# Dealing the row-maximum tiles of a cross-attention kernel otherwise over the steps of its windows

## The chip, the core and the metric

The kernel runs on one core of a Trainium2 chip. The time is device time in microseconds (us) of that core. Lower is better.

## What is computed

Two layers follow each other. The first, on `x` (8 sequences of 56 tokens of width 128) and a context (8 sequences of 1500 rows), is self-attention, cross-attention to the context, and a mixture of 8 experts with the best 2 of them chosen. The second is one more cross-attention to the same context, with weights rounded to three values. The core of both cross-attentions, with 16 heads of width 8, is:

```
k = context @ Wk.T + bk ; v = context @ Wv.T + bv        # 1500 rows for each of 8 sequences
scores = einsum('bqhd,bkhd->bhqk', q, k) * SCALE
probs  = softmax(scores, axis=-1)
out    = einsum('bhqk,bkhd->bqhd', probs, v)
```

## The kernel before, in words

All engines are programmed by hand, each with its own straight list of instructions, and wait for each other by semaphores. Each of the two cross-attentions is a *pass* over the 8 sequences (*units*). A pass has 8 *windows*, one for each unit, and a window has 12 *steps* k = 0 to 11. I write a window as (pass, unit): (0, 3) or (1, 0). Between the passes stand the experts.

In step k TensorE first computes one block of **scores** (`scores`, L1343, 8 matmuls into the PSUM tensor ST); ScalarE takes its exponential (`exp_step`, L671). In even steps TensorE then multiplies the exponentials of the two steps before with the **values** (`values`, L1386, 32 matmuls into PO).

The softmax needs the maximum of every score row ahead of the exponentials. So, one window ahead, the scores of the next unit are computed once more in rough form: 24 **max tiles** of 112 x 500 (`max_tile`, L1371). Each goes into one of the two banks of SM, and VectorE reduces it to its row maximum (`reduce_tile`, L883). A tile may only be computed when the reduction of the tile two before it is done. The tiles are numbered 0 to 23. How many stand in which step is the table `STEP_TILES`; the first window of all, (0, 0), has a table of its own, and the last window of each pass has no tiles. When tile 11 or tile 23 is reduced, `max_parts` makes the negated maxima of half the rows, and TensorE turns them (`transpose_max`, L1308) right after the scores of step 6 or of step 1.

Besides, a window prepares later units through one PSUM bank, MI. In steps 0, 1, 2 it projects the keys of the unit two ahead (`project_k`, L1282; thirds of 500 columns). ScalarE reads each third twice (`kf`, L635, then `ksplit`, L636), and the next third may be projected only after that. GpSimd then computes a rest (`k_rest`, L527), VectorE rounds it (`k_second_part`, L878, one in each of the steps 1, 2, 3), and GpSimd computes the third part (`k_third_part`, L532). In steps 4, 5, 6 the values of the next unit are projected (`project_v`, L1292). Step 7 turns the attention output back (`output_back`, L1318), which VectorE divides by the row sums in step 8 (L918). In pass 0, steps 9, 10, 11 transpose context (`transpose_ctx`, L1271, windows 0 to 4), and VectorE takes statistics of context in steps 5 to 10. In pass 1 the transposed context comes from HBM instead (`load_xT`, L368).

The three places for tiles within one step are: the first tile behind the values (behind the scores in odd steps), the middle ones directly behind it, the last one behind the projection.

SyncE's queue moves data between windows: `place` (L428) and `restack` (L412, six transfers that stack the rounded keys into `kst`), and `load_qall` (L393), which spreads the queries when they are split. A wait in this queue holds up all behind it.

Of the kernel before, what the change touches and what calls it, by code (L numbers as in the profile page):

```python
# [75 lines left out]
def spread_tiles(own, per):  # L76

    tiles = [(0, j) for j in range(TILES - own, TILES)] + [(1, j) for j in range(TILES)]
    assert sum(per) == len(tiles)
    return [tiles[sum(per[:k]):sum(per[:k + 1])] for k in range(STEPS)]  # L80
# [3 lines left out]

STEP_TILES = spread_tiles(0, (3, 3, 3, 2, 2, 2, 2, 2, 1, 1, 2, 1))
OWN_MX_STEP, NEXT_MX_STEP = 1, 6
# [5 lines left out]
OUT_AT, LN_AT, ROUTER_AT, GATES_AT, B2_AT = (5, 10), (6, 10), (6, 11), (7, 9), (7, 11)  # L92
LN5_AT, Q2_AT = (1, 3), (1, 9)
SPLIT2_AT = ((1, 10), (1, 11), (2, 0))
TERNARY_AT = ((4, 5), (4, 6), (4, 7), (4, 9), (4, 10), (4, 11), (5, 4), (5, 5), (5, 6), (5, 7), (5, 9))
# [77 lines left out]
def build_kernel(nc, x_in, ctx_in, ctxT_in, watt_in, vec_in, rows_in, rwT_in, w1T_in, w2T_in, b2_in,  # L173
                 ident_in, mask_in, out):
    with ExitStack() as ctx:
# [175 lines left out]
        def _(sp):  # L351
# [79 lines left out]
            def window(n):  # L431
# [4 lines left out]
                if n.s == 0 and n.c == B - 1:  # L436
                    restack(nxt, 1)
                if n.s == 0 and (n + 4).exists():
                    load_ctx(n + 4)
# [4 lines left out]
                if xT_unit is not None and xT_unit.s == 1:  # L444
                    load_xT(xT_unit)
                if n.s == 1 and n.c == 1:
                    load_qall(2)
                if n.s == 0 and n.c in (3, 4):
# [342 lines left out]
        def _(dve):  # L791
# [234 lines left out]
            def window(n):  # L1026
# [4 lines left out]
                for k in range(STEPS):  # L1031
                    tiles = n.tiles(k)
# [29 lines left out]
                    if n.s == 0 and (n.c, k) == GATES_AT:  # L1062
                        copy_gates(0)
                    if n.s == 1 and (n.c, k) == (0, 9):
                        token_stats(5)
                    if n.s == 1 and (n.c, k) == (0, 11):
                        token_normalise(5)
                    if n.s == 1 and (n.c, k) == LN5_AT:
                        token_gain(5)
# [127 lines left out]
        def _(pe):  # L1197
# [193 lines left out]
            def window(n, prev):  # L1391
# [3 lines left out]
                for k in range(STEPS):  # L1395
                    scores(n, k)
                    tiles = [(n + ahead, j) for ahead, j in n.tiles(k)]
                    if k % 2 == 0 and (k or prv.exists()):
                        of = n if k else prv
                        values(of, (k - 2) % STEPS)  # L1400
                        values(of, (k - 1) % STEPS)
                    if tiles:
                        max_tile(*tiles[0])
                    for tile in tiles[1:-1]:
# [271 lines left out]
```

## Time and profile before

| | us |
|---|---|
| three runs | 573.84, 576.63, 576.68 |
| median | 576.63 |
| the profiled execution | 574.07 |
| its span, first to last instruction | 572.3 |

| engine | busy, share of the span |
|---|---|
| TensorE (PE) | 90% |
| VectorE (DVE) | 68% |
| ScalarE (ACT) | 58% |
| GpSimd (POOL) | 39% |

TensorE's granted clock is 0.962 of full speed in the mean, and 1.00 in all the windows. PEld is TensorE's weight load, which overlaps the matmuls. A matmul's row gives its start and its duration to the last result; the next one starts earlier, so TensorE's time is best read from start to start.

### The profile page before, as it was taken

Reading aid. Unit: us, or ns where it says so; the run is one execution under the profiler, and the core shown is the slowest. Engines: PE = TensorE matmul, PEld = TensorE weight load, DVE = VectorE, ACT = ScalarE, POOL = GpSimd, SP = SyncE. Lnnn points to the kernel's source line nnn. Section 1 sums busy time; section 2 is a strip of 40 time slices with the busy share of each in tenths; the row PEclk is TensorE's granted clock in tenths of the full one; section 3 lists DMA queues with packets and bytes.
Section 4 is the critical chain, followed back from the end, with each engine's and each line's share of the span. In section 5 each row is a group of like instructions: output and inputs, shape, how many; then the busy total and the mean of one; then the engine's idle time right before and its main releaser. Section 6 shows DMA issues by size and latency. Waiting matters only on the chain.

```text
span 572.3 us, 16262 instructions
## 1 busy us (share of the span) xinstructions
PE 514.1 (90%) x6648; PEld 386.4 (68%) x6648; DVE 390.0 (68%) x976; ACT 334.4 (58%) x527; POOL 221.3 (39%) x217
## 2 busy tenths in 40 slices
PE   3599748889999999999989999999998999999996
PEld 2588515466767767676767998877666676766774
DVE  5666378788887888787741434887867777786730
ACT  1166223557676777776576444376666667675573
POOL 3659744475777768423160200031404033140000
PEclk9799677899999999999999999999999999999998
DMA  5110552634354554555638401006354835535200
GB/s 160 48 55 3 143 122 50 169 89 132 95 139 112 143 145 101 137 120 143 182 73 223 141 2 31 2 1 154 72 150 113 201 92 140 144 85 121 56 4 9
DMA packets 37869, 58.69 MB, mean 103 GB/s; under 512 B 17956, under 2 KB 21404, under 8 KB 37796
## 3 DMA queue, kind: packets, MB, share of 16 engines
q1 hardware_dynamic: 37476, 57.60, 39.8%
q8 instruction: 53, 0.87, 0.6%
q14 instruction: 20, 0.16, 0.1%
q10 hardware_dynamic: 320, 0.06, 0.1%
HBM read 17.81 MB, written 0.23 MB: 32 GB/s over the span
## 4 chain that ended last, share of the span: by engine, by line
PE 68%; DVE 17%; POOL 4%; DMA 3%; issue 3%; ACT 2%; SPq 2%; DVEq 0%; ACTq 0%; POOLq 0%
PE PO L1386 14%; PE SM L1371 14%; DVE mxp L883 11%; PE ST L1343 10%; PE MI L1292 8%; PE ST L1564 4%; PE ST L1554 4%; PE MI L1282 3%; PE MI L1271 2%; POOL cxs L518 2%; PE MI L1318 2%; DMA xT<-in_ctxT 1%; ACT pts L671 1%; PE SM L1477 1%; SPq L393 1%
## 5 line engine op out<-in xcount | busy, mean ns | idle before, releaser
L883 DVE TENSOR_REDUCE mxp<-SM 112x1 f32<-112x500 f32 x374 | 241.0, 673 | 74.4 <-PE SM L1371 73.2
L671 ACT ACTIVATE pts<-ST 128x896 f32<-128x896 f32 x192 | 171.7, 913 | 31.3 <-PE ST L1343 30.8
L1371 PE MATMUL SM<-kst,qst 96*112 96x500 bf16 x374 | 142.2, 399 | 13.0 <-DVE mxp L883 9.0
L527 POOL TENSOR_TENSOR kr<-kf,ksplit 128x500 f32<-128x500 f32 x48 | 55.1, 1150 | 172.4 <-ACT ksplit L636 172.4
L1343 PEld LDWEIGHTS ST<-qst,kst 98*128 98x128 bf16 x1536 | 95.8, 100 | 29.5 <-issue 4.7
L1343 PE MATMUL ST<-qst,kst 98*128 98x112 bf16 x1536 | 106.9, 213 | 2.6 <-DMA qst<-mrow 2.6
L1386 PE MATMUL PO<-pts,vaug 125*32 125x112 f32 x3072 | 97.3, 263 | 2.3 <-ACT pts L671 1.9
L1371 PEld LDWEIGHTS SM<-kst,qst 96*112 96x112 bf16 x374 | 45.6, 129 | 61.5 <-DVE mxp L883 45.0
L1386 PEld LDWEIGHTS PO<-pts,vaug 125*32 125x32 f32 x3072 | 69.3, 109 | 14.8 <-ACT pts L671 5.7
L518 POOL TENSOR_SCALAR cxs<-cxs,cmv,crstd 125x128 f32<-125x128 f32 x84 | 67.4, 819 | 0.0
L532 POOL TENSOR_TENSOR ksplit<-kr,ksplit 128x500 bf16<-128x500 f32 x48 | 54.4, 1135 | 16.9 <-DVE ksplit L878 16.9
L648 ACT ACTIVATE vaug<-MI 125x512 f32<-125x512 f32 x48 | 28.7, 598 | 53.1 <-PE MI L1292 53.1
L1292 PEld LDWEIGHTS MI<-watt,xT 128*125 128x125 f32 x384 | 50.6, 193 | 4.1 <-ACT vaug L648 1.4
L1292 PE MATMUL MI<-watt,xT 128*125 128x128 f32 x384 | 52.4, 281 | 1.1 <-DVE hT L827 0.8
L635 ACT ACTIVATE kf<-MI,vec 128x500 f32<-128x500 f32 x46 | 31.2, 678 | 36.0 <-PE MI L1282 35.7
L1282 PE MATMUL MI<-xT,watt 128*128 128x500 f32 x92 | 48.1, 604 | 1.5 <-ACT ksplit L636 0.8
L769 ACT ACTIVATE moe<-ST,vec 128x224 f32<-128x224 f32 x64 | 28.5, 448 | 34.8 <-PE ST L1554 33.9
L878 DVE CAST ksplit<-kr 128x500 bf16<-128x500 f32 x48 | 35.0, 729 | 10.2 <-POOL kr L527 10.1
L636 ACT ACTIVATE ksplit<-MI,vec 128x500 bf16<-128x500 f32 x46 | 30.8, 670 | 0.0
L623 ACT ACTIVATE xT<-MI,vec 128x500 f32<-128x500 f32 x24 | 18.4, 767 | 16.5 <-PE MI L1271 16.4
L506 POOL TENSOR_TENSOR xrstd<-xvar,half_neg 112x2 f32<-112x2 f32 (+1 forms) x6 | 4.9, 811 | 59.5 <-DVE xvar L809 59.5
L511 POOL TENSOR_TENSOR crstd<-cvar,half_neg 125x12 f32<-125x12 f32 x8 | 18.3, 2289 | 18.0 <-DVE cvar L865 18.0
(156 smaller groups left out, 539.8 us busy)
## 6 DMA issues: line engine op xcount, KB each, us to landing
kst<-ksplit SPq DMA_DIRECT2D x192, 187.5 KB, 3.6
cxs<-in_ctx SPq DMA_DIRECT2D x8, 750.0 KB
xT<-in_ctxT SPq DMA_DIRECT2D x8, 750.0 KB, 6.5
qst<-qall SPq DMA_DIRECT2D x56, 21.0 KB, 1.9
watt<-in_watt SPq DMA_DIRECT2D x1, 768.0 KB, 5.5
cxs<-in_w1T SPq DMA_DIRECT2D x3, 256.0 KB, 5.7
cxs<-in_w2T SPq DMA_DIRECT2D x3, 256.0 KB, 6.3
pts<-in_w1T SPq DMA_DIRECT2D x3, 256.0 KB, 5.4
```

What stands on the lines that cost most here:

```text
L518: last = nc.gpsimd.tensor_scalar(cx[n.par][:, c], cx[n.par][:, c], cmv[n.par][:, c, 0:1], crstd[n.par][:, c:c + 1], ALU.subtract, ALU.mult)
L527: nc.gpsimd.tensor_tensor(kr[:, c], kf[:, c], ksplit[n.par][:, 0, c], ALU.subtract).then_inc(kr_done, 1)
L532: nc.gpsimd.tensor_tensor(ksplit[n.par][:, 2, c], kr[:, c], ksplit[n.par][:, 1, c], ALU.subtract).then_inc(k3_done, 1)
L635: nc.scalar.activation(kf[:, c], bank[:, 0:THIRD], ACT.Identity, bias=bias_k(n.s + 1)).then_inc(k_evac, 1)
L671: nc.scalar.activation(PT[:, k % PTB], ST[:, k % 2, :, 0:4 * PC], ACT.Exp, scale=SCALE).then_inc(exp_done, 1)
L878: nc.vector.tensor_copy(ksplit[n.par][:, 1, c], kr[:, c]).then_inc(k2_done, 1)
L883: nc.vector.tensor_reduce(mxp[:, j // 3, j % 3:j % 3 + 1], tile_bank(j, banks), AX.X, ALU.max).then_inc(sm_red, 1)
L1282: mm(bank[:, 0:THIRD], watt[:, n.s + 1, 1], xT[n.par][:, THIRD * i:THIRD * (i + 1)], start=True, stop=True).then_inc(kp_full, 1)
L1292: last = mm(MI[0:KC, D * c:D * (c + 1)], xT[n.par][:, at:at + KC], watt[:, n.s + 1, 2], start=True, stop=True)
L1343: last = mm(ST[:, k % 2, cc, PC * p:PC * (p + 1)], kst[n.par][:, 4 * half + p, at:at + 128], qst[n.par][:, 4 * half + p], start=True, stop ...
L1371: mm(tile_bank(j, banks), qst[n.par][0:SROWS, j // 3], kst[n.par][0:SROWS, j // 3, at:at + THIRD], start=True, stop=True).then_inc(sm_full, 1)
L1386: last = mm(PO[32 * p:32 * p + 32, PC * half:PC * (half + 1)], vaug[n.par][:, c, at:at + 32], PT[0:KC, k % PTB, cc, PC * p:PC * (p + 1)], ...
```

## The change

Three things are changed, and nothing is computed otherwise.

1. The table: the 24 tiles are dealt 3, 2, 3, 1, 3, 2, 3, 2, 2, 1, 1, 1 to the steps, where they were dealt 3, 3, 3, 2, 2, 2, 2, 2, 1, 1, 2, 1. The table of window (0, 0) stays.
2. The order in a step: the first tile is computed ahead of the values, directly behind the scores. With at most three tiles in a step, one stands behind the scores, one behind the values and one behind the projection, where there are such.
3. In the second pass: the layer norm of the second half of the tokens, which precedes their query projection, moves from window (1, 1), step 3, to (1, 0), step 10, its parts on VectorE from steps 9 and 11 to 4 and 9; the query projection itself moves from (1, 1), step 9, to step 10; and SyncE issues `load_qall(2)` later, behind the first `restack` of window (1, 2) instead of at the end of window (1, 1).

```diff
--- before.py
+++ after.py
@@ -82,7 +82,7 @@
 
 
 
-STEP_TILES = spread_tiles(0, (3, 3, 3, 2, 2, 2, 2, 2, 1, 1, 2, 1))
+STEP_TILES = spread_tiles(0, (3, 2, 3, 1, 3, 2, 3, 2, 2, 1, 1, 1))
 OWN_MX_STEP, NEXT_MX_STEP = 1, 6
 FIRST_TILES = spread_tiles(TILES - START_TILES, (3, 3, 3, 3, 2, 2, 3, 3, 2, 2, 2, 2))
 FIRST_OWN_MX_STEP, FIRST_NEXT_MX_STEP = 3, 8
@@ -90,8 +90,8 @@
 
 
 OUT_AT, LN_AT, ROUTER_AT, GATES_AT, B2_AT = (5, 10), (6, 10), (6, 11), (7, 9), (7, 11)
-LN5_AT, Q2_AT = (1, 3), (1, 9)
-SPLIT2_AT = ((1, 10), (1, 11), (2, 0))
+LN5_AT, Q2_AT = (0, 10), (1, 10)
+SPLIT2_AT = ((1, 11), (2, 0), (2, 1))
 TERNARY_AT = ((4, 5), (4, 6), (4, 7), (4, 9), (4, 10), (4, 11), (5, 4), (5, 5), (5, 6), (5, 7), (5, 9))
 TAIL_BACK, TAIL_FORTH, TAIL_OUT, TAIL_LN, TAIL_ROUTER, TAIL_GATES, TAIL_B2 = 1, 3, 5, 9, 11, 18, 20
 TAIL_EXP, V0_PLACE = 15, 10
@@ -435,6 +435,8 @@
                     restack(n + 1, 1)
                 if n.s == 0 and n.c == B - 1:
                     restack(nxt, 1)
+                if n.s == 1 and n.c == 2:
+                    load_qall(2)
                 if n.s == 0 and (n + 4).exists():
                     load_ctx(n + 4)
                 if (n + 2).exists():
@@ -443,8 +445,6 @@
                     restack(k_unit, 0)
                 if xT_unit is not None and xT_unit.s == 1:
                     load_xT(xT_unit)
-                if n.s == 1 and n.c == 1:
-                    load_qall(2)
                 if n.s == 0 and n.c in (3, 4):
                     load_expert(n.c - 3)
                 if n.s == 0 and n.c >= 5:
@@ -1061,11 +1061,11 @@
                         router_gates(0)
                     if n.s == 0 and (n.c, k) == GATES_AT:
                         copy_gates(0)
+                    if n.s == 1 and (n.c, k) == (0, 4):
+                        token_stats(5)
                     if n.s == 1 and (n.c, k) == (0, 9):
-                        token_stats(5)
+                        token_normalise(5)
                     if n.s == 1 and (n.c, k) == (0, 11):
-                        token_normalise(5)
-                    if n.s == 1 and (n.c, k) == LN5_AT:
                         token_gain(5)
                     if n.s == 1 and (n.c, k) in SPLIT2_AT:
                         split_q(2, (SPLIT2_AT.index((n.c, k)),))
@@ -1395,12 +1395,12 @@
                 for k in range(STEPS):
                     scores(n, k)
                     tiles = [(n + ahead, j) for ahead, j in n.tiles(k)]
+                    if tiles:
+                        max_tile(*tiles[0])
                     if k % 2 == 0 and (k or prv.exists()):
                         of = n if k else prv
                         values(of, (k - 2) % STEPS)
                         values(of, (k - 1) % STEPS)
-                    if tiles:
-                        max_tile(*tiles[0])
                     for tile in tiles[1:-1]:
                         max_tile(*tile)
                     if 0 <= k - K_STEP < 3 and k_unit is not None:
```

On TensorE, steps 1 and 2 of window (0, 1), before. L1343 are scores, L1371 max tiles, L1282 the key projection, L1386 the values:

```order
L1343 MATMUL ST<-qst1,kst1 128x112 x8
L1308 MATMUL ST<-identb,mparts 8x112
L1371 MATMUL SM<-kst0,qst0 112x500 x2
L1282 MATMUL MI<-xT1,watt 128x500
L1371 MATMUL SM<-kst0,qst0 112x500
L1343 MATMUL ST<-qst1,kst1 128x112 x8
L1386 MATMUL PO<-pts,vaug1 32x112 x16
L1371 MATMUL SM<-kst0,qst0 112x500 x2
L1282 MATMUL MI<-xT1,watt 128x500
```

The same place after the change:

```order
L1343 MATMUL ST<-qst1,kst1 128x112 x8
L1308 MATMUL ST<-identb,mparts 8x112
L1371 MATMUL SM<-kst0,qst0 112x500
L1282 MATMUL MI<-xT1,watt 128x500
L1371 MATMUL SM<-kst0,qst0 112x500
L1343 MATMUL ST<-qst1,kst1 128x112 x8
L1371 MATMUL SM<-kst0,qst0 112x500
L1386 MATMUL PO<-pts,vaug1 32x112 x16
L1371 MATMUL SM<-kst0,qst0 112x500
L1282 MATMUL MI<-xT1,watt 128x500
```

Between the key projections of step 1 and step 2 the tiles now stand one by one; ahead of the projection of step 1 there is one tile where there were two.

On VectorE, steps 1 to 4 of window (0, 4), before. L878 are the three castings of the key rest in steps 1, 2, 3, L883 the reductions of the tiles, L889 the start of `max_parts`:

```order
L878 CAST ksplit<-kr 128x500
L883 TENSOR_REDUCE mxp<-SM 112x1 x3
L878 CAST ksplit<-kr 128x500
L883 TENSOR_REDUCE mxp<-SM 112x1 x2
L878 CAST ksplit<-kr 128x500
L883 TENSOR_REDUCE mxp<-SM 112x1 x2
L889 TENSOR_REDUCE nmx<-mxp 112x4
```

And after:

```order
L878 CAST ksplit<-kr 128x500
L883 TENSOR_REDUCE mxp<-SM 112x1 x3
L878 CAST ksplit<-kr 128x500
L883 TENSOR_REDUCE mxp<-SM 112x1
L878 CAST ksplit<-kr 128x500
L883 TENSOR_REDUCE mxp<-SM 112x1 x3
L889 TENSOR_REDUCE nmx<-mxp 112x4
```

Ahead of the third casting there is one reduction where there were two, and behind it, up to `max_parts`, there are three where there were two.

On SyncE's queue, at the seam of the windows (1, 1) and (1, 2):

```order
 L412 DMA kst<-ksplit 16x4x1500 x6
 L368 DMA xT<-in_ctxT 128x1500
-L393 DMA qall<-qsplit 16x8x224 x6
 L428 DMA qst<-qall 48x4x56 x2
 L412 DMA kst<-ksplit 16x4x1500 x6
+L393 DMA qall<-qsplit 16x8x224 x6
 L428 DMA qst<-qall 48x4x56 x2
```

The six issues of `load_qall` are moved past the two of `place` and the six of `restack`.

## Rows read from the trace of the kernel before

**Rows 1.** The page, chain of work that ended last: share of the span by engine.

```profile
PE 68%; DVE 17%; POOL 4%; DMA 3%; issue 3%; ACT 2%; SPq 2%; DVEq 0%; ACTq 0%; POOLq 0%
```

**Rows 2.** The waits: engine, line, waited for, us in total, times, longest.

```profile
PEld SM L1371 <- DVE mxp L883: 45.0, 119, 1.6
```

**Rows 3.** Timeline of window (0, 3), TensorE: start, us, instruction; in brackets idle before.

```profile
182.74 0.56 PE L1343 MATMUL ST<-qst,kst 98*128 98x112 bf16 x8
183.23 0.97 PE L1386 MATMUL PO<-pts,vaug 125*32 125x112 f32 x32
184.14 0.63 PE L1371 MATMUL SM<-kst,qst 96*112 96x500 bf16 x2
184.61 1.00 PE L1282 MATMUL MI<-xT,watt 128*128 128x500 f32 x2
...
190.22 1.00 PE L1282 MATMUL MI<-xT,watt 128*128 128x500 f32 x2
...
191.27 0.56 PE L1343 MATMUL ST<-qst,kst 98*128 98x112 bf16 x8
...
195.23 0.56 PE L1343 MATMUL ST<-qst,kst 98*128 98x112 bf16 x8
195.80 0.42 PE L1371 MATMUL SM<-kst,qst 96*112 96x500 bf16 x1
...
204.44 0.65 PE L1271 MATMUL MI<-ident,cxs 125*128 125x125 f32 x4 [0.64 <-DVE on L918]
...
208.74 0.46 PE L1343 MATMUL ST<-qst,kst 98*128 98x112 bf16 x6
```

**Rows 4.** Timeline of the same window, all engines, around its third key projection.

```profile
191.83 0.67 ACT L636 ACTIVATE ksplit<-MI,vec 128x500 bf16<-128x500 f32 x1
...
192.39 1.73 ACT L671 ACTIVATE pts<-ST 128x896 f32<-128x896 f32 x2
...
192.65 1.14 POOL L527 TENSOR_TENSOR kr<-kf,ksplit 128x500 f32<-128x500 f32 x1 [0.69 <-ACT ksplit L636]
...
193.75 1.14 POOL L532 TENSOR_TENSOR ksplit<-kr,ksplit 128x500 bf16<-128x500 f32 x1
193.82 1.33 DVE L878 CAST ksplit<-kr 128x500 bf16<-128x500 f32 x1 [0.17 <-POOL kr L527]
...
195.08 1.25 DVE L883 TENSOR_REDUCE mxp<-SM 112x1 f32<-112x500 f32 x2
```

**Rows 5.** Timeline of window (1, 4), TensorE: the scores of steps 0, 5 and next 0.

```profile
474.86 0.56 PE L1343 MATMUL ST<-qst,kst 98*128 98x112 bf16 x8
...
487.55 0.56 PE L1343 MATMUL ST<-qst,kst 98*128 98x112 bf16 x8
...
499.00 0.56 PE L1343 MATMUL ST<-qst,kst 98*128 98x112 bf16 x8
```

**Rows 6.** Timeline of the windows (1, 0) and (1, 1), all engines.

```profile
386.58 0.56 PE L1343 MATMUL ST<-qst,kst 98*128 98x112 bf16 x8
...
392.83 1.30 SPq L368 DMA_DIRECT2D xT<-in_ctxT  x1
...
400.33 1.08 PE L1282 MATMUL MI<-xT,watt 128*128 128x500 f32 x2 [0.70 <-DMA xT<-in_ctxT]
...
402.75 0.30 PEld L1282 LDWEIGHTS MI<-xT,watt 128*128 128x128 f32 x2 [0.23 <-ACT ksplit L636]
...
426.99 1.00 PE L1282 MATMUL MI<-xT,watt 128*128 128x500 f32 x2
```

**Rows 7.** Timeline of window (1, 2), all engines.

```profile
431.84 4.24 SPq L412 DMA_DIRECT2D kst<-ksplit  x6
...
439.25 0.39 PE L1371 MATMUL SM<-kst,qst 96*112 96x500 bf16 x1 [1.68 <-issue]
```

**Rows 8.** Timeline at the seam of windows (0, 0) and (0, 1).

```profile
130.76 0.56 PE L1343 MATMUL ST<-qst,kst 98*128 98x112 bf16 x8
...
131.06 1.26 DVE L883 TENSOR_REDUCE mxp<-SM 112x1 f32<-112x500 f32 x2
```

## The prediction

> **What bounds the kernel now.** The chain of work that ended last lies 68% on TensorE and 17% on VectorE [rows 1]. So TensorE is the bound, and VectorE stands in its way in places; the list of waits says where: weight loads of max tiles waited 45.0 us in 119 pieces for reductions [rows 2]. Part of that is hidden, since a weight load overlaps the matmul before it. What counts is read from start to start in the timeline.
>
> Window (0, 3) starts at 182.74 and the next at 208.74, a period of 26.00; its step 5 begins 12.49 after its start [rows 3]. In pass 1 the period is 24.14, and step 5 begins after 12.69 [rows 5]. TensorE's prices, from the same rows: scores and values together 1.40 (182.74 to 184.14), so about 0.49 for scores ahead of values and 0.91 for values; two tiles 0.47, so 0.24 each; a key projection with one tile 1.05. Scores ahead of a tile cost 0.40 (the tile at 195.80 stands 0.57 behind its scores, and 0.17 of that I read as waiting for a reduction). At 204.44 TensorE waited 0.64 for the division of step 8.
>
> Eleven windows are regular: (0, 1) to (0, 6) and (1, 2) to (1, 6). (0, 0) has its own table, (1, 0) and (1, 1) the layer norm, and the last of each pass no tiles.
>
> **The change part by part.** *The order and the table, first half of a window.* I walk through it with those prices, from the first scores at 0. Scores, tile, values, tile: 0.40 + 0.24 + 0.91 + 0.24 = 1.79, and the first key projection starts (before: 1.87). The second now has only scores, the turning of the maxima and one tile ahead of it, so TensorE is there early, but MI must be emptied first. The second reading starts 1.61 after a projection and takes 0.67 [rows 4], so this is possible 2.3 after the first one. The trace shows this limit once: at 402.75, 2.42 after the projection at 400.33, the weight load waited for ksplit [rows 6]. Hence 4.09. To the third: 1.05 + 0.40 + 0.24 + 0.91 + 0.24 = 2.84, hence 6.93. It was at 7.48 [rows 3], so 0.55 is gained so far.
>
> It is lost again on two other engines. ScalarE's exponentials of steps 3 and 4 start 2.17 after the third projection and take 1.73 together [rows 4], so the first is there at 10.0, while TensorE, with one tile in step 3, would want it 0.3 to 0.4 sooner. Then VectorE: it reaches the third casting with one reduction less behind it and has nothing to do until GpSimd has the rest ready; the casting then takes 1.33, since GpSimd's next instruction started 0.07 ahead of it, and the next reduction starts 4.86 after the third projection (190.22 to 195.08) [rows 4]. That does not move with the tiles. So the reduction of tile 9 starts at 11.79 and ends at 12.46, tile 11 starts at 12.50 where TensorE alone would be there at about 11.65, and step 5 begins at 12.74. That is 0.25 later than before in pass 0, 0.05 in pass 1.
>
> The Trainium skill, "SBUF — State Buffer", section "SBUF: two separate sides", says that VectorE and GpSimd share a port pair by an exclusive lock and that whichever instruction starts first holds it to its end. By that rule a casting that won the 0.07 us race would not be held at all; I make that a rival below, priced from rows.
>
> *Second half.* One tile moves there (12 stand ahead of step 5, where there were 13). In all it costs 0.24 of TensorE. The wait of 0.17 at 195.80 falls away. In pass 0 the 0.64 at 204.44 goes too, since two tiles and the values stand between; but VectorE has one more reduction there, beside its statistics, and I put new waits at 0.4 (bounds: 0, and the 0.64 itself). The sum is +0.07 in pass 1 and -0.17 in pass 0, where the context is transposed.
>
> So a regular window changes by +0.12 in pass 1 (five), +0.08 in (0, 1) to (0, 4), about +0.25 in (0, 5) and (0, 6), which have no transposes to gain from: 0.6 + 0.3 + 0.5 = **+1.4 us**. The bounds for one window: with no wait at all TensorE would be at step 5 after 11.1 (1.79, then 1.9 and 2.84 to the second and third projection, and 4.6 for one more with its tile, two scores, values, three tiles and a value projection), a gain of 1.4 to 1.6; if nothing is gained in the second half, loss 0.5.
>
> *The seam of (0, 0) and (0, 1).* Tiles of (0, 0) are still being reduced: VectorE starts two at 131.06 [rows 8]. Tile 0 now stands right behind the scores, at 131.16, and needs the first of these, done at 131.73. Formerly the values covered this. **+0.6**.
>
> *Layer norm and query projection.* From step 5 of (1, 0) at 386.58 to the first key projection of (1, 2) at 426.99 are 40.41 [rows 6]. After: step 5 0.25 later. The transfer of xT starts 6.25 after it and is waited for at 400.33, 13.75 after it; the transposes (0.4) and the tile (0.24) move into this stretch and fill the 0.70 of waiting, so it stays 13.75. From there one period of 24.26 and the query projection, some 0.5: 24.8. Sum 38.8, **-1.6**: the waits around the layer norm in (1, 1) are gone.
>
> *`load_qall`.* In (1, 2) a tile stood 1.68 idle until 439.25 [rows 7]; the profile names no engine. I take it for tile 12, the first to read the second half of kst, whose six transfers were issued from 431.84 to 436.08, late, since the queries' split and six issues of L393 stood ahead of them. Now they go ahead. **-1.7**. `load_qall` itself then waits for the last part of the split in step 1, and the queries are placed after step 5, with several us to spare.
>
> Sum: 1.4 + 0.6 - 1.6 - 1.7 = **-1.3**. On the profiled execution's 574.07 that is 572.8; the three runs lie at its level once and 2.6 above twice, so a median can fall at 572.8 or 575.4. I predict **574.0**, in its own range 570.5 to 577.5. A measurement of this kernel can tell about 0.5%, 2.9 us, from no change.
>
> **Rivals.** *The waits just go (faster).* For it speaks that VectorE is busy 68% only and that the reductions lie even now. TensorE alone would make step 5 after 11.1: 1.6 x 11 = 17.6 us less, about **555**. Against it stand the three waits worked out above, each on another engine than the one relieved. Chance 0.07.
>
> *The casting wins the race (faster).* VectorE now stands idle at the third casting. If it starts ahead of GpSimd's instruction, it takes about 0.4 and the reduction starts 0.9 sooner: 0.85 x 11 = 9.4 less than my sum, **563 to 565**. Against it: VectorE stood idle there before too (0.17) and lost by 0.07 [rows 4]. Chance 0.12.
>
> *VectorE falls behind and holds the turning of the maxima (slower).* In step 6 the turning now blocks a tile and the values. The maxima need tile 11's reduction, which ends at 13.6, and some 0.6 for their parts: 14.2. TensorE is there at 15.0 (12.74, two scores, two tiles and a value projection, which I price as a key projection, 0.8, plus the 0.1 that scores cost ahead of another kind). If VectorE is late by more than these 0.8, all that it is late counts: with 0.5 per window 5.5 us, **578.3 to 579**. For it speaks that GpSimd's normalising runs then in pass 0 and two more reductions are queued. Chance 0.15.
>
> *The transfer of xT becomes the bound of pass 1.* From step 5 to the first key projection there are 11.4 + 0.1 + 1.8 = 13.3 us, and the transfer was there after 13.75 at worst: 0.45 in up to three windows, 1.3 us, **574 to 575.5**. It only adds to the forecast; chance 0.06, within "same".
>
> **Chances.** The forecast has 0.60, of which 0.08 lie beyond 0.5% on the fast side and 0.02 on the slow side. Faster 0.08 + 0.07 + 0.12 = 0.27, rounded 0.28; slower 0.02 + 0.15 = 0.17; same the rest, 0.55. The range leaves out the first rival and half of what lies beyond the others: 565 to 579.
>
> **What would show it.** In the profile of the changed kernel a regular window should be 26.1 long in pass 0 and 24.3 in pass 1. The second key projection should start 2.3 after the first, held by ksplit. The values of step 4 should wait for the exponentials. VectorE should wait for GpSimd's rest, cast in 1.3, and tile 11 should wait some 0.8. The total waiting of weight loads for reductions should fall well below 45 us, with the span hardly shorter: the waits are relabelled, not removed. The 1.68 and the waits at 400 to 421 should be gone. I am wrong if the period falls by more than 0.3, if the third casting is short, or if the waiting in (1, 2) stays.

## The result and the profile after

The changed kernel took 580.26 us in the median of 9 runs (577.5 to 586.92), the kernel before 576.63 (9 runs); the ratio is 1.0055, 95% interval 1.003 to 1.008. The prediction was 574.0. Measured once more on another chip it took 577.66 (12 runs) beside 578.91 (23 runs): 0.9997, 0.9962 to 1.0032. So the two measurements leave room for anything from a gain of 0.4% to a cost of 0.8%. The 1.3 us that the sum of the prediction gained (0.2%) are excluded by the first interval and lie inside the second; the 2.6 us by which 574.0 stands below the kernel before lie outside both. The medians are of all runs, while the ratios leave out executions disturbed by a lower granted clock, of which the first profiled one was one (586.90; lower in the first 60 us and in window (0,0)). From window (0,1) to the end of the first pass its periods agree with those of the second profiled execution (581.12) within 0.02 us.

In what follows "start" of a window is the start of its step 0; a "period" runs from one start to the next.

The page of the changed kernel, chain of work that ended last, which answers to [rows 1]: TensorE has less of it, GpSimd, ScalarE and "issue" more.

```profile
PE 65%; DVE 13%; POOL 6%; ACT 5%; issue 5%; DMA 3%; SPq 2%; POOLq 0%; ACTq 0%; DVEq 0%
```

The waits for reductions (engine, line, waited for, us in total, times, longest) fell from the 45.0 of [rows 2]:

```profile
PEld SM L1371 <- DVE mxp L883: 28.5, 73, 1.7
```

Timeline of window (0,3) after, TensorE, which answers to [rows 3] (start, us, instruction, idle before):

```profile
194.60 0.56 PE L1343 MATMUL ST<-qst,kst 98*128 98x112 bf16 x8
195.00 0.38 PE L1371 MATMUL SM<-kst,qst 96*112 96x500 bf16 x1
195.31 0.97 PE L1386 MATMUL PO<-pts,vaug 125*32 125x112 f32 x32
196.21 0.42 PE L1371 MATMUL SM<-kst,qst 96*112 96x500 bf16 x1
196.47 1.00 PE L1282 MATMUL MI<-xT,watt 128*128 128x500 f32 x2
...
198.81 1.10 PE L1282 MATMUL MI<-xT,watt 128*128 128x500 f32 x2 [0.24 <-ACT ksplit L636]
199.75 0.38 PE L1371 MATMUL SM<-kst,qst 96*112 96x500 bf16 x1
...
201.82 1.00 PE L1282 MATMUL MI<-xT,watt 128*128 128x500 f32 x2
...
204.97 0.59 PE L1386 MATMUL PO<-pts,vaug 125*32 125x112 f32 x16 [0.19 <-ACT pts L671]
...
207.40 0.42 PE L1371 MATMUL SM<-kst,qst 96*112 96x500 bf16 x1 [0.61 <-DVE mxp L883]
207.66 0.56 PE L1343 MATMUL ST<-qst,kst 98*128 98x112 bf16 x8
...
216.94 0.65 PE L1271 MATMUL MI<-ident,cxs 125*128 125x125 f32 x4
...
221.04 0.56 PE L1343 MATMUL ST<-qst,kst 98*128 98x112 bf16 x8
```

The period is 26.44, not 26.00. Step 5 stands 13.06 after the start (12.49 before), the rest takes 13.38 (13.51 before; the 0.64 at the transposes is gone). The third key projection is reached after 7.22 (before 7.48), and from it to step 5 are 5.84 (before 5.01). All of the loss is in that second stretch. The other two engines there, answering to [rows 4]:

```profile
204.25 1.13 POOL L527 TENSOR_TENSOR kr<-kf,ksplit 128x500 f32<-128x500 f32 x1 [0.69 <-ACT ksplit L636]
205.34 1.13 POOL L532 TENSOR_TENSOR ksplit<-kr,ksplit 128x500 bf16<-128x500 f32 x1
205.42 1.34 DVE L878 CAST ksplit<-kr 128x500 bf16<-128x500 f32 x1 [0.75 <-POOL kr L527]
206.68 0.67 DVE L883 TENSOR_REDUCE mxp<-SM 112x1 f32<-112x500 f32 x1
```

VectorE, with one reduction less, stands idle for 0.75 ahead of the third casting, is held in it for 1.34, and the reduction that TensorE needs starts at 206.68.

The second pass, window (1,2), answering to [rows 5]: period 24.70 (24.14 in (1,4) before), step 5 after 13.05.

```profile
437.34 0.56 PE L1343 MATMUL ST<-qst,kst 98*128 98x112 bf16 x8
...
450.39 0.56 PE L1343 MATMUL ST<-qst,kst 98*128 98x112 bf16 x8
...
462.04 0.56 PE L1343 MATMUL ST<-qst,kst 98*128 98x112 bf16 x8
```

One window comes out the other way. In (1,6), the last one with tiles, no keys are left to project, and so there are no castings either. Its scores of step 0 and of step 5 are 12.13 apart before and 9.64 after, and the whole window takes 23.49 before and 21.37 after. The timelines, before and then after:

```profile
524.99 0.56 PE L1343 MATMUL ST<-qst,kst 98*128 98x112 bf16 x8
...
537.12 0.56 PE L1343 MATMUL ST<-qst,kst 98*128 98x112 bf16 x8
```

```profile
539.63 0.56 PE L1343 MATMUL ST<-qst,kst 98*128 98x112 bf16 x8
...
549.27 0.56 PE L1343 MATMUL ST<-qst,kst 98*128 98x112 bf16 x8
```

Step 5 of (1,0) and the first key projection of (1,2), answering to [rows 6], are 38.82 apart (40.41 before); the wait of [rows 7] in (1,2) is gone.

```profile
400.38 0.56 PE L1343 MATMUL ST<-qst,kst 98*128 98x112 bf16 x8
...
439.20 1.00 PE L1282 MATMUL MI<-xT,watt 128*128 128x500 f32 x2
```

The seam of (0,0) and (0,1), answering to [rows 8]; from the scores (140.99) to the first key projection (143.59) are 2.60, where they are 1.87 before:

```profile
142.11 0.39 PE L1371 MATMUL SM<-kst,qst 96*112 96x500 bf16 x1 [0.56 <-DVE mxp L883]
```

What [rows 6] only hinted at is at the start of window (1,4). SyncE issues the transfer of xT behind 5.41 us of key copies, and the projection waits. The timeline of the first, then of the second profiled execution of the changed kernel:

```profile
477.04 5.41 SPq L412 DMA_DIRECT2D kst<-ksplit  x6
482.49 0.95 SPq L368 DMA_DIRECT2D xT<-in_ctxT  x1
...
490.15 1.08 PE L1282 MATMUL MI<-xT,watt 128*128 128x500 f32 x2 [1.39 <-DMA xT<-in_ctxT]
```

```profile
467.18 5.97 SPq L412 DMA_DIRECT2D kst<-ksplit  x6
473.19 0.89 SPq L368 DMA_DIRECT2D xT<-in_ctxT  x1
...
482.10 2.01 PE L1282 MATMUL MI<-xT,watt 128*128 128x500 f32 x2 [3.20 <-DMA xT<-in_ctxT]
```

### The profile page after: what moved, and what is told of

It reads as the page before. It is cut to its first block, busy times and chain, and to the rows that moved or that the text cites. A ratio compares the mean times of both kernels' runs of the same rounds, so it can differ in the third digit from the quotient of the medians.

```text
span 585.1 us, 16262 instructions
## 1 busy us (share of the span) xinstructions
PE 526.4 (90%) x6648; PEld 393.9 (67%) x6648; DVE 391.7 (67%) x976; ACT 333.5 (57%) x527; POOL 220.5 (38%) x217
## 4 chain that ended last, share of the span: by engine, by line
PE 65%; DVE 13%; POOL 6%; ACT 5%; issue 5%; DMA 3%; SPq 2%; POOLq 0%; ACTq 0%; DVEq 0%
PE SM L1371 12%; PE PO L1386 12%; PE ST L1343 9%; PE MI L1282 7%; PE MI L1292 5%; DVE mxp L883 5%; PE ST L1564 4%; PE ST L1554 4%; DVE ksplit L878 3%; POOL kr L527 3%; ACT ksplit L636 3%; PE SM L1477 2%; PE MI L1271 2%; POOL cxs L518 2%; DMA xT<-in_ctxT 1%
## 5 line engine op out<-in xcount | busy, mean ns | idle before, releaser
L883 DVE TENSOR_REDUCE mxp<-SM 112x1 f32<-112x500 f32 x374 | 242.9, 674 | 67.5 <-PE SM L1371 65.9
L1371 PE MATMUL SM<-kst,qst 96*112 96x500 bf16 x374 | 147.7, 400 | 13.8 <-DVE mxp L883 12.3
L1343 PEld LDWEIGHTS ST<-qst,kst 98*128 98x128 bf16 x1536 | 95.9, 100 | 34.9 <-issue 11.8
L1343 PE MATMUL ST<-qst,kst 98*128 98x112 bf16 x1536 | 107.7, 214 | 2.0 <-DMA qst<-mrow 2.0
L1386 PE MATMUL PO<-pts,vaug 125*32 125x112 f32 x3072 | 98.7, 264 | 4.3 <-ACT pts L671 3.8
L1386 PEld LDWEIGHTS PO<-pts,vaug 125*32 125x32 f32 x3072 | 70.1, 110 | 29.3 <-issue 17.4
L1371 PEld LDWEIGHTS SM<-kst,qst 96*112 96x112 bf16 x374 | 48.3, 130 | 46.1 <-DVE mxp L883 28.5
L532 POOL TENSOR_TENSOR ksplit<-kr,ksplit 128x500 bf16<-128x500 f32 x48 | 54.3, 1133 | 16.8 <-DVE ksplit L878 16.8
L1282 PE MATMUL MI<-xT,watt 128*128 128x500 f32 x92 | 49.8, 624 | 4.8 <-ACT ksplit L636 3.4
L878 DVE CAST ksplit<-kr 128x500 bf16<-128x500 f32 x48 | 35.0, 728 | 16.9 <-POOL kr L527 16.8
```

Source lines behind the costliest of these rows:

```text
L532: nc.gpsimd.tensor_tensor(ksplit[n.par][:, 2, c], kr[:, c], ksplit[n.par][:, 1, c], ALU.subtract).then_inc(k3_done, 1)
L878: nc.vector.tensor_copy(ksplit[n.par][:, 1, c], kr[:, c]).then_inc(k2_done, 1)
L883: nc.vector.tensor_reduce(mxp[:, j // 3, j % 3:j % 3 + 1], tile_bank(j, banks), AX.X, ALU.max).then_inc(sm_red, 1)
L1282: mm(bank[:, 0:THIRD], watt[:, n.s + 1, 1], xT[n.par][:, THIRD * i:THIRD * (i + 1)], start=True, stop=True).then_inc(kp_full, 1)
L1343: last = mm(ST[:, k % 2, cc, PC * p:PC * (p + 1)], kst[n.par][:, 4 * half + p, at:at + 128], qst[n.par][:, 4 * half + p], start=True, stop ...
L1371: mm(tile_bank(j, banks), qst[n.par][0:SROWS, j // 3], kst[n.par][0:SROWS, j // 3, at:at + THIRD], start=True, stop=True).then_inc(sm_full, 1)
```

## The experiments

All runs below are measured beside the kernel before on the same chip. "Pass 0" is the sum of the six periods from (0,1) on, "pass 1" of the five from (1,0) on, each from first key projection to first key projection in the profiled execution; "K2 to S5" is the stretch from the third key projection to step 5 in window (0,3), "xT" the wait of a key projection for xT in the second pass. What each kernel changes is said below the table.

| kernel | median us | ratio (95%) | pass 0 | pass 1 | K2 to S5 | xT |
|---|---|---|---|---|---|---|
| before | 576.6 to 578.9 | 1 | 154.33 | 125.46 | 5.01 | 0.70 |
| changed | 580.26 | 1.0055 (1.003 to 1.008) | 156.67 | 126.00 | 5.84 | 1.39 |
| after_again | 577.66 | 0.9997 (0.9962 to 1.0032) | 156.72 | 130.39 | 5.84 | 3.20 |
| old_table | 573.69 | 0.9936 (0.9905 to 0.9968) | 154.54 | 121.68 | 5.35 | 0 |
| old_order | 580.75 | 1.005 (1.0006 to 1.0095) | 157.30 | 127.97 | 5.83 | 2.28 |
| moves_only | 572.44 | 0.9925 (0.989 to 0.9959) | 154.32 | 121.76 | 5.01 | 0 |
| late_cast | 571.29 | 0.9897 (0.9849 to 0.9946) | 153.18 | 121.46 | 5.01 | 0 |
| pool_waits | 569.29 | 0.9893 (0.9842 to 0.9944) | 152.29 | 120.72 | 5.02 | 0 |
| two_tiles | 574.40 | 0.996 (0.9926 to 0.9995) | 154.32 | 122.84 | 5.35 | 0.25 |
| late_old_table | 574.18 | 0.995 (0.9918 to 0.9983) | 154.56 | 122.47 | 5.35 | 0.57 |
| old_table_free | 574.71 | 0.9937 (0.9908 to 0.9965) | 154.54 | 121.68 | 5.35 | 0 |
| moves_free | 572.79 | 0.9889 (0.9841 to 0.9936) | 153.80 | 121.34 | 5.01 | 0 |
| first_old (one run) | 578.41 | | 156.73 | 125.55 | 5.84 | 0.58 |
| early_xT | 609.37 | 1.0557 (1.0502 to 1.0612) | 159.99 | 150.24 | 5.83 | 0 |
| xT_gpsimd | 592.61 | 1.0251 (1.0203 to 1.03) | 167.15 | 126.45 | 5.83 | 0 |
| pool_waits_xT | 589.01 | 1.0197 (1.0141 to 1.0253) | 162.24 | 129.01 | 5.01 | 0 |
| moves_free_xT | 586.21 | 1.0144 (1.0101 to 1.0187) | 164.91 | 123.16 | 5.02 | 0 |
| xT_gpsimd2 | 588.25 | 1.0155 (1.01 to 1.021) | 156.68 | 132.98 | 5.83 | 0 |
| pool_waits_xT2 | 575.40 | 0.9907 (0.9864 to 0.9949) | 152.29 | 125.50 | 5.01 | 0 |

Medians of different rows come from different chips; the ratios are what compares.

**Which part loses.** The change has three parts: the table, the order (tile ahead of the values), and the moves in the second pass. Each of these three kernels takes one or two back.

```
old_table:  STEP_TILES = spread_tiles(0, (3, 3, 3, 2, 2, 2, 2, 2, 1, 1, 2, 1))
old_order:  max_tile(*tiles[0]) again behind the two values(...)
moves_only: both of these
```

> The changed kernel with the tiles dealt as before the change (3, 3, 3, 2, 2, 2, 2, 2, 1, 1, 2, 1); the new order in a step and all moves of the second pass stay. Theory A, the table costs and the order gains: with two tiles in step 3 VectorE has a reduction to do while it waits for the third casting, so tile 11 waits 0.3 instead of 0.6, and with three tiles in step 1 the second key projection is hardly held by ksplit. The period of a regular window falls from 26.4 to about 25.6 in pass 0 and from 24.8 to about 23.7 in pass 1, some 0.8 to 1.0 in each of 11 windows: about 570 us, 1% faster than the kernel before. Theory B, the order costs (a lone tile ahead of the values delays them, and its reduction now gates them), the table is neutral: periods stay at 26.4 and 24.8, about 580 us.

> The changed kernel with the first tile behind the values again; the new table and all moves of the second pass stay. Theory A: the table alone is the loss, periods 26.4 and 24.8 or a little longer, about 580 us, not faster than the changed kernel. Theory B: with the order of before the periods fall back to 26.0 and 24.2, and with the moves it is some 3 us faster than the kernel before, about 574 us.

> The kernel before with the moves of the second pass alone (layer norm, query projection, the issue of the queries' spreading); table and order as before. Both theories: the 1.68 us idle in window (1, 2) goes, and 1.6 around the layer norm; 3.3 us less than the kernel before, about 573.5 us, periods of the regular windows as before. A rival for this part: a window that is sooner through catches up with the transfer of xT, and half of it comes back as a wait for that transfer, 575 us.

The moves alone give 3.7 us in pass 1 (125.46 to 121.76) and a ratio of 0.9925. The order with the old table changes nothing that can be told (0.9936). The new table brings the loss back with either order (1.005 and 1.0055). So theory A of old_table was right that the table costs, but its size was not: it hoped for periods of 25.6 and got 26.1. In (1,6), without castings, both parts gain: from step 0 to step 5 are 12.13 in moves_only, 10.68 with the new order alone (old_table), 11.25 with the new table alone (old_order) and 9.64 with both. In window (0,3) of old_table VectorE has a second tile of step 3 to reduce ahead of the casting, and step 5 comes 5.35 after the third projection:

```profile
193.51 1.00 PE L1282 MATMUL MI<-xT,watt 128*128 128x500 f32 x2
...
195.50 0.42 PE L1371 MATMUL SM<-kst,qst 96*112 96x500 bf16 x1 [0.16 <-DVE mxp L883]
...
198.86 0.56 PE L1343 MATMUL ST<-qst,kst 98*128 98x112 bf16 x8
```

**Is it the third casting?** Two kernels take the casting's hold away from the tile in different ways: behind the first reduction of step 4, or left where it is but with no GpSimd operation beside it.

```diff
 late_cast (VectorE)
+                    if k == K_STEP + 4 and k_unit is not None:
+                        k_second_part(k_unit, 2)
...
-                    if 0 <= k - K_STEP - 1 < 3 and k_unit is not None:
+                    if 0 <= k - K_STEP - 1 < 2 and k_unit is not None:
 pool_waits (GpSimd, k_parts)
                 k_rest(n, 2)
+                pool.wait_ge(k2_done, n.count(3, 3))
                 k_third_part(n, 1)
```

> The changed kernel with VectorE's third casting moved from step 3 to behind the first reduction of step 4. Theory A: VectorE reduces tile 9 while it would stand idle for GpSimd, so tile 11 does not wait its 0.6 and the period falls by about 0.6 in each of 13 windows: about 573 us. Theory B: the casting does not bound, about 580 us as the changed kernel.

> The changed kernel; in GpSimd's work on the next keys the third part of the second third waits until VectorE has finished the third casting, so that the casting has no 1.13 us GpSimd operation beside it; its order on VectorE is kept. Theory A (the third casting's 1.34 us, of which about 0.9 is a wait for GpSimd, holds back the reductions of the first half and with them the pace of TensorE): the casting takes about 0.4 us, periods of regular windows fall from 26.4 to 25.4 to 25.9 in the first pass and from 24.7 to 23.7 to 24.2 in the second, time 568 to 573. Rival B (what late casting gained came from the reduction order, not from the shorter casting): the casting is short but the periods stay at 26.4, time 578 to 581. Rival C: the keys' third parts come later by the wait, the copies of the keys and xT transfer follow later, and the wait for xT grows to over 2 us in some windows; time 574 to 577.

Both take away the 0.83 lost between K2 and S5 (5.01 and 5.02 for 5.84), and both kernels are faster than the kernel before. Timeline of pool_waits, VectorE, GpSimd and TensorE in the same place:

```profile
195.52 0.42 DVE L879 CAST ksplit<-kr 128x500 bf16<-128x500 f32 x1 [0.75 <-POOL kr L527]
195.85 1.96 DVE L884 TENSOR_REDUCE mxp<-SM 112x1 f32<-112x500 f32 x3
196.02 2.23 POOL L532 TENSOR_TENSOR ksplit<-kr,ksplit 128x500 bf16<-128x500 f32 x2 [0.53 <-DVE ksplit L879]
...
196.94 0.56 PE L1344 MATMUL ST<-qst,kst 98*128 98x112 bf16 x8
```

The casting takes 0.42 for 1.34, and no tile waits for a reduction in the first half; the 0.19 for the exponential stays. In late_cast it is as long as ever, but nobody waits behind it:

```profile
199.15 1.34 DVE L878 CAST ksplit<-kr 128x500 bf16<-128x500 f32 x1 [0.17 <-POOL kr L527]
...
200.56 0.56 PE L1345 MATMUL ST<-qst,kst 98*128 98x112 bf16 x8
```

**Does the hold cost something with the old table?**

> The changed kernel with the old table (3, 3, 3, 2, 2, 2, 2, 2, 1, 1, 2, 1) and the third casting of the keys behind the first reduction of step 4: the two edits that were each faster alone. Theory A: they take away the same wait (reductions late behind the third casting), so they do not add: periods 25.6 to 25.9 and 23.7 to 24.2, time 569.5 to 571.5. Rival: they add in full (573.7 and 571.3 against 580.3 give 6.6 and 9.0), time 564 to 567.

> The changed kernel with the old table and the third casting free of GpSimd's operation beside it. Theory A as for the kernel with the moves: nothing, periods 26.1 and 24.4, time 573 to 574.5. Rival B: with the casting free, both tables are alike or the old one is ahead: periods 25.6 or below, time 566 to 569. The same edit with the new table gave 25.7 and 24.0 and 569.3.

> The kernel before with the moves of the second pass, and with the third casting free of GpSimd's operation beside it (GpSimd's third part of the second third waits for the third casting); the old table and the old order, values ahead of the tile. Theory A (the hold matters only where VectorE comes to the casting with tiles waiting behind it, which the new table with its single tile in step 3 brings; with the old table late_old_table gained nothing over old_table): periods within 0.1 of the 25.98 and 24.4 of the kernel with the moves alone, time 571.5 to 573. Rival (every blocked casting costs its 0.9 us): periods 25.1 to 25.6, time 562 to 568.

With the old table neither edit shortens the stretch from K2 to S5: 5.35 as in old_table, 5.01 as in moves_only. The periods are those of old_table (26.1 in pass 0), but for one wait of 0.57 for xT in late_old_table; in moves_free they are 0.1 shorter than in moves_only (25.9 for 26.0). late_old_table thus met neither of its expectations: its two edits together gain nothing over old_table. (Its casting takes 0.98, since it starts later and ends where it ended before.) So in these kernels a held casting costs much only where the reduction behind it is the one that TensorE needs next. Without the hold the new table is the better one by the profiled periods: pass 0 is 152.29 against 154.54 with the old table in the same order. The ratios, 0.9893 and 0.9937, have intervals that overlap.

**The single tile of step 3.**

```
two_tiles: STEP_TILES = spread_tiles(0, (3, 2, 3, 2, 2, 2, 3, 2, 2, 1, 1, 1))
```

> The changed kernel with the table 3, 2, 3, 2, 2, 2, 3, 2, 2, 1, 1, 1: one max tile moved from step 4 to step 3. Theory A (VectorE has work to spare in steps 1 to 3 and is behind from the third casting on, so that tiles dealt earlier give it its maxima earlier): the tiles behind step 3 wait less, periods 25.7 in the first pass and 23.9 to 24.3 in the second, time 571 to 575. Rival (the tiles of all steps wait for the buffers of the maxima alike, whichever step they are dealt to): periods within 0.1 of 26.4 and 24.8, time 579 to 581.

The period falls from 26.44 to 26.05 and K2 to S5 from 5.84 to 5.35, as with the old table; 25.7 was hoped for. A second tile in step 3 gives half of what the free casting gives, since it waits itself: it starts 0.54 behind the first (195.26 and 195.80 in the timeline of two_tiles), where a tile behind a tile costs 0.24.

**The seam and a second profile.**

```
first_old: in (0, 0), and in step 0 of the window behind it, the tile stands behind the values
```

> The changed kernel with the values ahead of the tile in window (0,0) and in the first step behind it, as before; all other windows in the new order. The prediction's step on the seam (the tile set ahead of the last values of window (0,0) waits some 0.6 us there): the wait of 0.56 us at the start of window (0,1) goes, and with it 0.5 to 0.6 us between the last key projection of (0,0) and the first of (0,1); the rest stays at 26.4. Rival: the wait stays, at another tile. Sum 0.6 us under the changed kernel, about 579.7.

> The changed kernel itself once more, for an execution whose start is not disturbed and for a second measurement of the disputed size. If the loss lies in the windows and not in the start: the same periods as in the first profile (26.44 in the regular windows of the first pass, 126.0 in sum in the second), the first key projection of window (0,0) at 101 to 106 instead of 109.6, ratio 1.003 to 1.008, time 579 to 581. Rival (part of the loss was that one execution's): periods or xT wait differ by over 0.3 in sum, ratio under 1.002.

In first_old the wait of 0.56 is gone: the timeline has the values at 134.80 and two tiles at 135.71 with no idle time. Its one run took 578.41; a difference of 0.6 cannot be read from that. after_again repeats the first pass to 0.05 us in sum, and puts a larger wait for xT into the second. Its ratio of 0.9997 and its 4.4 us more in pass 1 are what its rival expected: a part of the first measurement belonged to those executions.

**The wait for xT.** Three edits tried to take it away.

```diff
 early_xT (SyncE, window)
+                if xT_unit is not None and xT_unit.s == 1:
+                    load_xT(xT_unit)
                 if (n + 2).exists():
                     place(n + 2, 0)
                 if k_unit is not None:
                     restack(k_unit, 0)
 xT_gpsimd (GpSimd, end of window; xT_gpsimd2: ahead of token_rstd(2))
+                if xT_unit is not None and xT_unit.s == 1:
+                    pool.wait_ge(vp_full, (xT_unit + -2).count(3, 3))
+                    nc.gpsimd.dma_start(xT[xT_unit.par][:], src).then_inc(ld_xT[xT_unit.par], 16)
```

> The changed kernel; on SyncE the transfer of xT is issued ahead of the placing of queries and the first half of the key copies of the same window, not behind them. Theory: in the seam of windows (1,3) and (1,4) the matmuls waited 1.39 us for xT, whose issue stood behind 5.4 us of key copies; ahead of them it is issued earlier and the wait goes, if its own condition (the value projection of the unit two back) is met by then: periods of the second pass fall by 1.4 in sum, time 578 to 579.5. Rival: the condition is met only late, the copies of the keys queue behind the transfer, and the scores wait for the keys instead: time 581 to 590.

> The changed kernel; in the second pass GpSimd, behind its work on the keys, issues the transfers of xT on its own queue, with the same condition, instead of SyncE behind the placing and the key copies. Theory (the waits for xT, 3.20 and 1.39 us in two executions of the changed kernel, come because SyncE issues the transfer 5.0 to 6.0 us of key copies late, and they are not worked into its windows): no wait for xT; periods of the second pass 24.8, 25.2, 24.7, 24.8, 25.0, sum 124.5 against 130.4 and 126.0; time 1.5 to 5 us under the changed kernel on the same chip, 573 to 577. Rival A (the transfer and the key copies share the DMA engines, so both land later whoever issues them): the wait for xT stays or the scores wait for keys, no gain. Rival B (issuing on GpSimd costs VectorE or GpSimd time): the third parts of the keys come later, periods above 25.

> The changed kernel with the third casting free of GpSimd's operation beside it and xT issued by GpSimd in the second pass. The free casting alone gave 569.3 and periods of 24.0 to 24.4 in the second pass with no wait for xT. Theory: with no wait left for xT to take away, the same periods within 0.2, time 568.5 to 570. Rival: xT waits in other executions than the profiled one made part of the 569.3, time 566.5 to 568.

> The kernel before with the moves of the second pass, the third casting free, and xT issued by GpSimd. Theory: as without the last edit (572.8, periods 25.9 and 23.5 to 25.0), the one long period of 25.02 in the second pass falling to 24.4 if it was a wait for the transfer of queries or xT; time 571.5 to 573. Rival: 569 to 571.

> The changed kernel with xT issued by GpSimd as in xT_gpsimd, but in window (0,5) ahead of the layer norm's reciprocal roots, behind which the first transfer left late there and cost one wait of 8.37 us. Theory: that wait goes, the last windows of the first pass are 26.4 and 24.8 again, and the second pass stays without a wait for xT (126.5 in sum, as in xT_gpsimd): 576 to 579. Rival A: the second pass stays at 126.5 and so no gain over the execution of the changed kernel with 126.0: the wait for xT is worth nothing in the usual execution, 579 to 581. Rival B: the transfer on GpSimd's queue lands late in the last windows of the first pass too (landing 7.5 us in the median against 6.5), 583 to 590.

> The changed kernel with the third casting free, and xT issued by GpSimd with its place mended as in xT_gpsimd2. With xT issued by SyncE the free casting gave 569.3 and a second pass of 24.0 to 24.4 per window without a wait for xT; with xT on GpSimd it was 24.0 to 26.7. Theory: the key copies and the transfer meet in the second pass, so that this stays at 569.3 or above, 569 to 575. Rival: 566.5 to 568.5.

early_xT was the rival, and dearer than it: the transfer's own condition, the last value projection at 461.40, holds the whole queue of SyncE; the key copies leave at 464.27, 2.87 behind the start of that projection, where the changed kernel sends them 1.88 ahead of it (452.39 and 454.27), and TensorE waits 3.35. The profile names no releaser, but the last of the six copies is issued at 468.3 and takes 4.6 to land, and the tile starts at 473.07.

```profile
461.40 1.04 PE L1292 MATMUL MI<-watt,xT 128*125 128x128 f32 x8
462.47 0.33 SPq L368 DMA_DIRECT2D xT<-in_ctxT  x1
...
464.27 5.12 SPq L412 DMA_DIRECT2D kst<-ksplit  x6
...
473.07 0.64 PE L1371 MATMUL SM<-kst,qst 96*112 96x500 bf16 x1 [3.35 <-issue]
```

On GpSimd's queue the transfer left late once, in (0,5), behind reciprocal roots that waited 14.88 for VectorE, and a projection waited 8.37. In xT_gpsimd, pool_waits_xT and moves_free_xT pass 0 is 10 to 11 us longer than in the same kernel without the edit. In pool_waits_xT pass 1 is 8.3 longer besides (129.01 for 120.72). The timeline of xT_gpsimd:

```profile
267.14 0.72 POOL L504 TENSOR_TENSOR xrstd<-xvar,half_neg 112x2 f32<-112x2 f32 x1 [14.88 <-DVE xvar L812]
267.82 0.78 POOL L569 DMA_DIRECT2D xT<-in_ctxT  x1
...
275.70 2.01 PE L1285 MATMUL MI<-xT,watt 128*128 128x500 f32 x2 [8.37 <-DMA xT<-in_ctxT]
```

With that mended, xT_gpsimd2 took 588.25 (ratio 1.0155), slower than the changed kernel, with no wait for xT anywhere in its second pass of 132.98. (xT_gpsimd, alike in the second pass, had 126.45 there: this too varies from one execution to another.) The wait went over to a tile. GpSimd issues xT at 476.51, and it lands 9.3 later; SyncE issues the six key copies from 473.25 on. The first four land after 3.2 to 4.2, the next after 6.5, and the last, issued at 477.3 right behind xT, after 10.2, at 487.5, which is when the tile starts. The timeline, and the row for the last copy:

```profile
473.25 5.23 SPq L412 DMA_DIRECT2D kst<-ksplit  x6
...
487.53 0.64 PE L1374 MATMUL SM<-kst,qst 96*112 96x500 bf16 x1 [4.03 <-issue]
```

```profile
DMA to landing us min/median/max: 10.2/10.2/10.2
```

pool_waits_xT2 took 575.40 (ratio 0.9907), pass 1 125.50 where pool_waits has 120.72. So in the second pass xT and the key copies get in each other's way, and in these runs whichever was put ahead made the other late. How much of the changed kernel's time the wait for xT makes is therefore not settled by taking it away. What stands is that it was there in all four profiled executions in which the new table met the held casting (old_order 2.28, changed 1.39, after_again 3.20, first_old 0.58); of the eight others with the moves made and SyncE's queue unchanged, two_tiles had 0.25, late_old_table 0.57, six had none.

## Why the prediction was wrong

*The first half of a regular window, to the third key projection* was mis-sized. Predicted 6.93 after the start, measured 7.22. The limit at 2.3 by the second reading was right (2.34, waiting for ksplit). The tile between scores and values costs 0.31 to the values (195.00 to 195.31), not the 0.24 of two tiles in a row, and it stands there twice; a key projection that had to wait takes 0.94 to the next tile (198.81 to 199.75), not 0.84; from it to the third are 3.01, not 2.84. Those prices were taken from rows with other neighbours. Of the 0.36 by which a window of (0,1) to (0,3) is longer than forecast (+0.44 for +0.08), 0.29 are in this stretch.

*From there to step 5* the forecast was 5.81 and 5.84 was measured, with each piece named: the exponential (0.19), VectorE with nothing to do ahead of the casting, the casting held for 1.34 (1.33 forecast), tile 11 late (0.61). Here the working was right, and pool_waits and late_cast show the cause: without the hold the stretch is 5.02.

*The second half*: 13.34 forecast, 13.38 measured; the 0.64 went as said. In the second pass 11.52 forecast, 11.65 measured.

*The steps that failed* are the term "regular windows +1.4" and the wait for xT, which the sum had at nothing. Behind the first stands mainly the stretch to the third key projection, priced at 6.93 where it took 7.22. From the start of (0,1) to the end of the span are 441.54 before and 444.11 in the first profiled execution of the changed kernel, 2.57 more where the sum had 1.3 less. The difference of 3.9 is made up thus:

| | forecast | measured |
|---|---|---|
| (0,1) to (0,6) | +0.82 | +2.34 |
| (1,2) to (1,4), without the waits of rows 7 and for xT | +0.36 | +1.92 |
| (1,5) and (1,6) | +0.24 | +0.80 and -2.12 |
| seam | +0.6 | +0.73 |
| (1,0) and (1,1) | -1.6 | -1.09 |
| wait of rows 7 (load_qall) | -1.7 | -1.68 |
| wait for xT | 0 | +1.39 |
| from the start of (1,7) on | 0 | +0.28 |

Ten windows with key projections thus cost 5.1 where 1.3 was forecast. (1,6) was counted among the regular ones though it projects no keys, and its 2.12 hide a part of that loss. The seam was sized by its wait alone, which was 0.56 as forecast. For (1,0) and (1,1) the 38.82 seem to meet the 38.8 of the prediction, but that is luck: the 38.8 were counted from the old step 5 and held 0.25 for its delay, while the 38.82 start at the new step 5, which itself comes 0.50 later after the first key projection (11.18 for 10.68). The moves of the second pass together gave 3.7 for 3.3 in moves_only.

The forecast of 574.0 also lies midway between 572.8 and 575.4, which are the sum taken off the profiled execution (574.07) and off the median (576.63); so another 1.3 of the miss of 6.3 us come from the level. In the second profiled execution the same stretch is 7.0 longer than before, by its wait for xT and what came behind it; the rest of the miss in the medians is not accounted for.

*The wait for xT* was put at 0.45 in each of up to three windows, from one landing 13.75 after step 5, with a chance of 0.06 and as nothing in the sum. In after_again it landed 8.8 after its issue at 473.19, 16.8 after step 5 (465.23). Between the placing of queries and the next key projection there is as much time as with the old table: 24.77 less 11.86 (465.82 less 453.96) is 12.9, in old_table 24.14 less 11.29 also 12.9. It is the copies (5.97 for 4.43 to issue) and the transfer (8.8 for 6.1 to land) that took longer. I had carried over one execution's duration as if it were a bound, where it was one draw. Why the copies take longer in some executions stays open.

*Rivals.* The casting did not win the race, though VectorE stood idle for 0.75: it waits for the very instruction on whose end GpSimd's next one starts, so idle time does not help it (205.34 against 205.42). In the changed kernel GpSimd's instruction is 0.07 to 0.08 ahead in every window from (0,1) on. The Trainium skill, "SBUF — State Buffer", section "SBUF: two separate sides", says that whichever starts first holds the lock of the shared port pair to its end; the rows agree, 1.34 with a GpSimd operation ahead and 0.42 without. The waits did not just go, except in (1,6). VectorE was not late for the turning of the maxima: TensorE shows no idle time ahead of it. The slower outcome of the first measurement came by a way that had no rival of its own: the windows' own price, and a wait for xT of 1.39 in one window where the rival for it had 0.45 in each of three.

## What to carry to other kernels

Suppose an engine has to wait for an operation's input. If you take away the work that fills this idle time, the operation does not start sooner; the work comes behind it instead, and late. When tiles are dealt anew, look at which one the first reduction behind such an operation belongs to. Here one wait of 0.53 us on GpSimd, which had time, freed VectorE's casting and gave the new table the shortest passes of the study (152.29 and 120.72, ratio 0.9893). By the ratios it cannot be told from moves_free (0.9889), late_cast (0.9897) or moves_only (0.9925), which shows how little of it a median can see. A price goes with its neighbours and with what the window holds: check that each window counted as regular has all the work of the one that was priced. And a transfer that one profile shows landing just about when it is needed has nothing to spare: look at its spread over executions before pricing it.

## What was not expected of the hardware

A wait of 3.20 us cost more than itself. The stretches of after_again around it (us, busy time of each engine, granted clock, DMA share, GB/s) show the granted clock at 1.00 before, 0.72 in the wait and 0.50, the lower of the two levels (1.2 GHz), for 4 us behind it; the projections of 1.0 us took 2.01 and 1.87, and the period behind the wait was 27.47, where the first execution, with 1.39 of waiting and the clock at 1.00 throughout, has 25.05. After the wait of 2.28 in old_order the clock stayed at 1.00 too.

```profile
474.00:478.00 4.00, 4.00 (x84) 2.97 (x85) 2.57 (x5) 2.94 (x5) 0.00 (x0) 1.00 0.77 234
...
480.00:482.00 2.00, 0.00 (x0) 0.00 (x0) 0.00 (x0) 0.00 (x0) 0.00 (x0) 0.72 0.71 186
482.00:484.00 2.00, 1.90 (x3) 0.82 (x4) 0.00 (x0) 0.00 (x0) 0.00 (x0) 0.50 0.96 218
484.00:486.00 2.00, 2.00 (x13) 1.38 (x12) 0.68 (x1) 1.75 (x4) 0.47 (x1) 0.50 0.30 72
```

The length of window (0,0) was between 29.81 and 34.34 in these profiled executions, and its first key projection started between 101.9 and 109.6, in no order that follows the edits: a single profiled time of this kernel says little below 5 us, and the periods say more.
